# Scaling expert weights on GpSimd: one multiplication, or two in the same instruction

## The reference

```
h   = patches @ proj_w.T + proj_b                            # 768 -> 192
xq  = fake_quant(layernorm(h))                                # 4 bit
q, k, v = split(xq @ fake_quant(ww1).T)                       # 12 heads of 64
a   = softmax(fake_quant(q) @ fake_quant(k).T / 8)            # 36x36 per head and image
o   = fake_quant(a) @ fake_quant(v)
h   = h + fake_quant(o) @ fake_quant(ww2).T + bb2
xn  = layernorm(h)
e   = argmax(xn @ Wg + bg)                                    # one of 4 experts per token
h   = h + gelu(xn @ W1[e] + b1[e]) @ W2[e] + b2[e]            # 192 -> 768 -> 192
```

## Time and profile before

| | us |
|---|---|
| median of 3 runs (218.57 to 219.69) | 219.22 |
| the profiled execution, its own time | 218.28 |
| its span | 216.5 |
| VectorE busy | 151.9 |
| GpSimd busy | 88.3 |
| TensorE busy | 165.3 |
| ScalarE busy | 120.7 |

### The profile page before, as it was taken

The page is one execution under the profiler, slowest core; times in us unless marked ns, Lnnn a source line. Parts: engine busy times, 40 slices in busy tenths (PEclk is TensorE's granted clock), DMA queues, the critical chain, the costliest instruction groups (busy, mean ns, idle before and its releaser), DMA issues.

```text
span 216.5 us, 5230 instructions
## 1 busy us (share of the span) xinstructions
PE 165.3 (76%) x1822; PEld 116.2 (54%) x1822; DVE 151.9 (70%) x446; ACT 120.7 (56%) x219; POOL 88.3 (41%) x114
## 2 busy tenths in 40 slices
PE   0796993687779998995486780896189999999970
PEld 0785882344555555654354660874056666666640
DVE  3175488779999989999997257991255655666670
ACT  8834761399987687897666358043024444444520
POOL 2021216908983773559371131885010332222223
PEclk9999999599965558599555555699659999999998
DMA  5899504999330120021012000314670000000000
GB/s 152 286 266 319 218 3 149 287 218 357 96 109 3 16 97 3 0 54 58 3 15 100 0 0 0 113 73 150 179 274 8 20 11 18 29 18 21 3 21 19
DMA packets 9464, 20.38 MB, mean 94 GB/s; under 512 B 1744, under 2 KB 5210, under 8 KB 9440
## 3 DMA queue, kind: packets, MB, share of 16 engines
q1 hardware_dynamic: 8288, 17.38, 27.1%
q0 software_dynamic: 1152, 2.68, 3.5%
HBM read 14.99 MB, written 5.35 MB: 94 GB/s over the span
## 4 chain that ended last, share of the span: by engine, by line
PE 37%; DVE 28%; issue 11%; DMA 9%; POOL 6%; SPq 3%; ACT 3%; DVEq 0%; POOLq 0%; ACTq 0%
PE lin_bank L1098 12%; PE head_bank L1110 7%; DMA patches<-in_patches 6%; POOL slots L417 5%; PE lin_bank L906 3%; DVE mx L694 2%; PE head_bank L1111 2%; DVE oT L588 2%; DVE den L697 2%; DVE aq L588 2%; DVE q L588 2%; DVE dif L702 2%; DMA patches<-slots 2%; PE lin_bank L910 2%; PE head_bank L879 2%
## 5 line engine op out<-in xcount | busy, mean ns | idle before, releaser
L551 ACT ACTIVATE q<-lin_bank,b 128x128 f32<-128x128 f32 x72 | 26.5, 368 | 46.9 <-PE lin_bank L1098 36.5
L1098 PE MATMUL lin_bank<-q,w 128*128 128x128 f16 (+1 forms) x360 | 39.9, 227 | 0.0
L1098 PEld LDWEIGHTS lin_bank<-q,w 128*128 (+1 forms) x360 | 26.9, 99 | 13.4 <-issue 1.7
L423 POOL DMA_INDIRECT out<-q,patches x12 | 14.2, 1183 | 48.6 <-DVE q L843 48.3
L516 ACT ACTIVATE oint<-head_bank,fac 64x432 int16<-64x432 f32 x32 | 19.7, 615 | 7.8 <-PE head_bank L963 7.4
L1110 PE MATMUL head_bank<-early,q 128*128 x72 | 23.3, 341 | 0.3 <-DVE q L861 0.3
L859 DVE CAST q<-q 128x384 f16<-128x384 f32 x24 | 8.7, 362 | 17.8 <-ACT q L551 17.8
L879 PE MATMUL head_bank<-proj_w,patches 128*128 128x192 f32 x72 | 14.4, 357 | 8.3 <-DMA patches<-in_patches 8.3
L910 PE MATMUL lin_bank<-xqT,ww1q 96*128 96x288 bf16 x96 | 19.6, 351 | 1.4 <-ACT qkint L468 0.7
L929 PE MATMUL score_bank<-k,q 128*128 128x36 bf16 x256 | 9.8, 188 | 13.3 <-DVE dif L702 8.6
L389 POOL TENSOR_SCALAR patches<-patches 128x768 f32<-128x768 f32 x8 | 17.6, 2200 | 5.7 <-DMA patches<-in_w 5.5
(11 more groups left out here) (137 smaller groups left out, 349.2 us busy)
## 6 DMA issues: line engine op xcount, KB each, us to landing
patches<-in_patches SPq DMA_DIRECT2D x9, 384.0 KB, 12.0
slots<-blank SPq DMA_DIRECT2D x12, 194.0 KB, 8.9
patches<-slots SPq DMA_DIRECT2D x12, 194.0 KB, 4.2
patches<-in_w SPq DMA_DIRECT2D x4, 576.0 KB, 3.9
early<-in_ww SPq DMA_DIRECT2D x3, 576.0 KB, 11.2
patches<-in_w SPq DMA_DIRECT2D x1, 1536.0 KB, 8.0
patches<-in_w SPq DMA_DIRECT2D x2, 768.0 KB, 12.6
proj_w<-in_proj_w SPq DMA_DIRECT2D x1, 576.0 KB, 4.3
```

Source lines behind the costliest of these rows:

```text
L551: a.activation(g[:, j % 2, m], up_bank[n % 4][:, 0:P], ACT.Gelu, scale=1.0 / WSCALE, bias=b1[:, bass.ds(e, 1), m]).then_inc(g_ok, 1)
L1098: last = mm(up_bank[n % 4][:, 0:P], we, xT[0:rows, j % 3, piece], start=x == 0, stop=x == len(PASSES) - 1)
```

## The change

The scaling instruction gets a second operation: the weight is multiplied by 64 and the product by 1. The result is the same number. All eight executions of line 389 change; nothing else does, and no instruction on any engine is moved.

```diff
             def split(n):
                 w, whi, wlo = split_views(n)
-                gp.tensor_scalar(w, w, WSCALE, None, ALU.mult).then_inc(wscaled, 1)
+                gp.tensor_scalar(w, w, WSCALE, 1.0, ALU.mult, ALU.mult).then_inc(wscaled, 1)
                 pool.wait_ge(wscaled, n + 1)
```

## The result

| | before | after |
|---|---|---|
| median of 4 runs, us | 218.89 | 221.84 |
| ratio to before | | 1.0127 (1.0091 to 1.0162) |
| profiled execution: its time, its span | 218.28, 216.5 | 221.12, 219.4 |
| L389, mean ns | 2200 | 858 |
| GpSimd busy, us | 88.3 | 77.6 |

A forecast was written before the change was run, and what follows sets the result against it. VectorE was taken as the bound from 49 to 113 us. Lateness 0 and collisions 0 left the profiled execution at 218.28 us, which is 219.2 on the median; the range was 216.4 to 222.4.

The forecast's parts named there:

- the one road: 49 to 113 us: L389 can move the end only through GpSimd's collisions with VectorE, which loses 11.8 us there.
- lateness: First term: a longer L389 delays inverse roots and last weights; zero up to a doubling, and a shorter one gains nothing.
- the collisions: Second term: GpSimd lengthening VectorE's instructions on the shared memory path; from -2.8 to +5.2 us, 0 at the value taken.
- The duration of the new form: Time of the two-operation L389 on GpSimd: between 1.03 and 4.40 us, taken as 2.20 us, no change.
- the nearest row, its own: L389's own present 2.20 us, taken as the time of the two-operation form.
- my lower bound: Shortest time allowed for the new L389: 1.03 us, the mean of GpSimd's cast of the same 768 columns.
- the likeliest case: No change: L389 keeps 2.20 us; 219.2 us on the median, own range 218.6 to 219.9, chance 0.36.
- Quicker form, dearer collisions: Rival: shorter L389 moves cast and subtraction onto `dens` and `aint` in four turns; 2.8 us slower, 222.0, chance 0.17.
- The excess of 14 us or so: Sign of a quicker form with a loss: VectorE's time above least durations, 49 to 113 us, rising from 11.8.
- The price per us of GpSimd: In the pieces: 11.8 us lost by VectorE over 39.9 us of busy GpSimd, 0.30 us per us.
- a gain of up to 2.8 us: Rival of a quicker form with fewer collisions: up to 2.8 us, middle 2.1, 217.1 on the median, chance 0.30.
- The longer form: Rival: L389's second operation is its own pass, 0.6 us each; +1.4 us, 220.6 on the median, chance 0.17.

The follow-up runs named there:

- e7: Kernel before, with L389 as multiply by 64, then maximum with -3e38, on all 768 columns; 222.18 us, ratio 1.0160.
- e4: Kernel before plus a memset and eight scalings of a spare tile, in various operations, at GpSimd's idle end; 234.39 us with them, single execution.
- e3: Changed kernel, with GpSimd's cast in pieces 3 to 7 waiting for VectorE's clip `aq`; 218.01 us, ratio 0.9951 to the kernel before.
- e6: Kernel before (one operation), with GpSimd's cast in the last five pieces waiting for VectorE's clip `aq`; 217.71 us, ratio 0.9952.
- e9: Changed kernel, with GpSimd's cast waiting for VectorE's clip `aq` in all eight pieces; 216.91 us, ratio 0.9945 to the kernel before.
- e10: As e9, but in pieces 4, 6 and 7 the cast waits for `aint`, one instruction earlier; 220.57 us, ratio 1.0093 to the kernel before.
- e2: Kernel before, with the two multiplications only in the last five pieces (3 to 7); 222.15 us, ratio 1.0108.
- e5: Kernel before, with the one-operation L389 on 256 of the 768 columns, two thirds of W1 left unscaled; 221.59 us, ratio 1.0113.
- e1: Kernel before, with the two multiplications only in the first three pieces (0 to 2); 218.92 us, ratio 0.9976.
- e8: Changed kernel, with the cast of pieces 3 to 7 done by ScalarE instead of GpSimd; 219.80 us, ratio 1.0075 to the kernel before.

## Why the prediction was wrong, point by point

- **The bound, and the one road.** Right. VectorE is the bound from 49 to 113 us (busy 62.3 of 64 us in the changed kernel), lateness is zero in both directions (the changed kernel and e7), and the collisions in five turns sum to 2.86 us of the 2.9 that the span grew by.
- **The duration of the new form.** This is the step that failed. Between 1.03 and 4.40 us I took "the nearest row, its own", 2.20, with the reason that the fixed way of going through the data dominates. It takes 0.86, below even my lower bound, which was a mean with collisions in it; the cast takes 0.82 at least. How long the way through the data takes depends on the operations (e4), so it was not fixed. That the instruction took 2.14 us where the cast takes 0.82 was a sign that a quicker way may exist on this engine, and I read it as a sign for no change.
- **The choice among cases.** With the duration went the likeliest case. "Quicker form, dearer collisions" had 0.17 and was what happened. Its mechanism held: `dens` under the cast, `aint` under the subtraction for 1.3 us, `xn` given back 0.6 us. Its sum did not. It had left the 0.56 us of `dens` out, and so said 0.7 us a turn for 1.13, and it counted four turns like the earlier trace rows. They are alike in how `oT` is held, but one of them had `aq` and `xn` held already and so lost nothing; three lose, and two give back 0.53 us together. The two errors cancel: 4 x 0.7 = 2.8 us forecast, 3 x 1.13 - 0.53 = 2.86 on the ruler and 2.95 between the medians. That this rival's 222.0 us lies beside the measured 221.84 is therefore in part luck. The excess of 14 us or so that was named as its sign came out at 15.1.
- **The price per us of GpSimd.** 0.30 us of VectorE per us of GpSimd made a gain of up to 2.8 us out of a shorter instruction. It has the wrong sign. e3 and e6 show no difference between 0.9 and 2.2 us of L389 at the same places, and e9 and e10 differ by 1.5% with instructions of the same length. The price is per place, not per us.
- **The longer form**, priced at +1.4 us, measured 1.6% (1.1 to 2.1), about 3.5 us. The size given to the instruction was too low to begin with: it grew by 1.14 us eight times and not by 0.6, and at 0.30 us per us that would be 2.7 us, inside the interval. So this run alone does not speak against the rule.
- **What I had seen in the trace and not weighed**: L389 left `dens` and `aint` alone in its middle. A shorter instruction moves the cast and the subtraction into that place (the changed kernel, e2 and e5). It was written under the rival and should have set its chance.

## What to carry to other kernels

An engine off the critical path that shares a path to memory with the one that sets the pace can be charged by where its instructions fall, and, as here, hardly by how long they are; before making one quicker, walk through what moves up behind it and onto what. A wait that pins such work to a quiet place can be worth more than a quicker instruction, and an edit of one place should be tried with it. An instruction that takes far longer than another over the same data is worth measuring in its neighbouring forms at the idle end of the program.

## What was not expected of the hardware

- On GpSimd, float32 in place, 128x768, alone: multiply 2.16 us, add 2.15, multiply and multiply 0.84, multiply and add 0.84, add and subtract 2.79, max and min 2.79 (e4, one execution). Multiply and maximum took 2.78 us at least (e7). Adding a multiplication by 1 makes a scaling 2.5 times as quick.
- The slow one-operation form leaves VectorE's instructions alone in its middle in most turns (`dens` at 0.22 and `aint` at 0.46 us beside it in the earlier trace rows), while cast and subtraction hold them to their own end. Not in every turn: in the kernel before, this `dens` came 1.47 us after the start of an L389 (77.59 to 79.82) and was held to 79.85, just past its end. What decides it stays open.

```profile
79.06 0.79 DVE L717 TENSOR_SCALAR dens<-den,quant 108x8 f32<-108x8 f32 x1
```

- Profiled executions differ by about 1 us ahead of the stage that was changed: the third maximum of the loop (`mx`) starts at 48.41 us in the kernel before, at 48.23 in the changed one, and at 49.38 in e7, where the granted clock of 40 to 49 us was 0.52 instead of 0.79, near the lower of its two levels (1.2 of 2.4 GHz) for all of the stretch. The same low clock (0.50 to 0.57) stands in the traces of e1 to e4, e8 and e10, and in these and e7 the third `mx` starts 8.6 us after the second, in the others 7.7 to 7.9. That is up to 0.8 us ahead of the changed stage, in kernels with the change and without it.
